# Converting weights to bf16 in HBM before they are streamed, and moving their loads from POOL to SP

## The chip, the cores and the metric

The kernel runs on the 8 cores of one Trainium2 chip, the same program on each. The metric is the device time in microseconds of the slowest core.

## What is computed

One transformer layer on x of shape (2, 4096, 4096) in float32: grouped-query attention with 32 query heads and 8 key/value heads of width 128, whose keys and values go through a narrow projection; then a feed-forward part with one dense 4096x4096 matrix and a top-2 mixture of 28 rank-8 adapters. Cut to what matters:

```python
def attn(u):
    q = heads(u @ Wq.T)                       # Wq 4096x4096
    kc, vc = u @ Wk_down.T, u @ Wv_down.T     # 4096 -> 256 each
    lat = interleave(kc, vc)                  # then k, v = up-projections
    k, v = lat[..., :256] @ Wk_up.T, lat[..., 256:] @ Wv_up.T
    p = softmax(causal(q @ k.T / sqrt(128)))
    return (p @ v) @ Wo.T                     # Wo 4096x4096
def ffn(u):
    logits = u @ gate_W.T                     # 28 experts, top 2
    h = (u @ lora_A.T) * gate(logits) * 2.0   # 28 x 8
    return u @ base_W.T + h @ lora_B.T        # base_W 4096x4096
x = x + layernorm(attn(layernorm(x)))
x = x + layernorm(ffn(layernorm(x)))
```

## The kernel before

Each core handles one of the two sequences together with three others, and owns 1024 of its 4096 rows as two halves of 512. It computes the compressed keys and values of all 4096 rows itself. All weights arrive as float32 in HBM, already laid out in blocks: WQ4 and WO4 as 32 blocks of [128, 4096], BWBM4 (base_W with lora_B appended) as 32 of [128, 4352], ATP (lora_A) as 32 of [128, 256], WKVD4 as 4 of [128, 4096]. Every such load is issued by POOL (`GPS`) and casts to bf16 on the way into SBUF. Waits are written out by hand on semaphores, and each engine runs its program in order.

The work has these stages:
- Keys and values, lines 247 to 283: eight blocks `ub` of 512 rows. For each: four tiles of X, layer norm on VectorE and ScalarE (`ln_stats_apply`, into the two-deep buffer UTM), four 1 MB transposes issued by SP (`tr_u`, L210) into UFMA or UFMA2; then `pa_loads(ub + 1)` queues the next X loads on POOL (L245); then four column groups `cg`, each a 1 MB WKVD4 load on POOL (L270) into WP[cg % 2] and 32 matmuls of 512 columns (L274), evacuated by VectorE.
- Then for each half `ci` of the own rows: layer norm and transposes of XOWN (L315, L323), Q projection over 32 groups `hdc` (load L330, matmuls L334), attention (L348 to L500), output projection over 32 groups `oc2` (load L540, matmuls L544) whose results SP transposes back (`tp_out2`, L534), two layer norms, gate, 32 small ATP loads with 4 matmuls each (L659, L665), and the FFN over 32 groups (load L709, 34 matmuls at L713 and L718, `tp_ffn` L703), with a last layer norm and the stores of OUT by SP (L754).

In all the weight loops the buffers WP[0] and WP[1] alternate: a load waits until the matmuls of the group two before it are done (`wp_free`), and the matmuls wait for the load. HSC is transposed by SP in four small transposes (L691) between the ATP loop and the FFN loop.

Of the kernel before, what the change touches and what calls it, by code (L numbers as in the profile page):

```python
# [7 lines left out]
BF16 = mybir.dt.bfloat16  # L8
# [51 lines left out]
def build(nc, do_b=True, do_c=True, dbg=False, dbg_stage=None):  # L60
# [4 lines left out]
    WQ4 = nc.dram_tensor("WQ4", [32, 128, 4096], F32, kind="ExternalInput").ap()  # L65
# [4 lines left out]
    WO4 = nc.dram_tensor("WO4", [32, 128, 4096], F32, kind="ExternalInput").ap()  # L70
    BWBM4 = nc.dram_tensor("BWBM4", [32, 128, 4352], F32, kind="ExternalInput").ap()
    GWT = nc.dram_tensor("GWT", [128, 896], F32, kind="ExternalInput").ap()
    ATP = nc.dram_tensor("ATP", [32, 128, 256], F32, kind="ExternalInput").ap()
    OUT = nc.dram_tensor("OUT", [1024, DM], F32, kind="ExternalOutput").ap()

    DBGT = None
    if dbg:
        DBGT = nc.dram_tensor("DBG", [512, DM], F32, kind="ExternalOutput").ap()
# [22 lines left out]
    WP = [A("WPa", [128, 34 * 128], BF16, O_WS), A("WPb", [128, 34 * 128], BF16, O_WP1)]  # L101
# [30 lines left out]
    TEN, VEC, SCA, GPS, SYN = nc.tensor, nc.vector, nc.scalar, nc.gpsimd, nc.sync  # L132

    tS = Sem(nc, "tS")
# [5 lines left out]
    sWPh = [Sem(nc, "sWPh0"), Sem(nc, "sWPh1")]  # L140
# [6 lines left out]
    sAP = [Sem(nc, "sAP0"), Sem(nc, "sAP1")]  # L147
    sST = Sem(nc, "sST")
    sSTp = [Sem(nc, "sSTa"), Sem(nc, "sSTb")]
    sRES = Sem(nc, "sRES")  # L150


    def W(eng, *sv):
        for s, v in sv:
            if v > 0:
                eng.wait_ge(s.h, v)
# [50 lines left out]
    def tr_u(dst, tspan, toff, utile, waits, pb):  # L207
# [4 lines left out]
    all_dma_sems = sXA + [sWPs[0], sWPs[1], sWPh[0], sWPh[1],  # L212
                    sTU[0], sTU[1], sTH[0], sTH[1],
                    sTP, sTHR, sWKV, sGW[0], sGW[1], sAP[0], sAP[1], sST, sRES,
                    sSTp[0], sSTp[1]]

    def final_waits():
        for s in all_dma_sems:
            if s.v > 0:
                SYN.wait_ge(s.h, s.v)  # L220


    Xr = X.rearrange("(q0 eight) d -> q0 eight d", eight=8)
    xu_extra = []
# [9 lines left out]
    wp_free = [0, 0]  # L234
# [13 lines left out]
    for ub in range(8):  # L248
        ubuf = UFMA if ub % 2 == 0 else UFMA2
        for t4 in range(4):  # L250
            pb = (ub * 4 + t4) % 6
            pl = (ub * 4 + t4) % 2
            xm = pend_xm[t4]
            xt = xa_tile(pb)
            ut = UTM[:, pl * 4096:(pl + 1) * 4096]
            ap_mark, red_mark = ln_stats_apply(
                xt, ut, pl,
                waits_v=[(sXA[pb], xm)],
                waits_s=[(sXA[pb], xm), (sTU[pl], utm_free[pl])])
            free_xa[pb] = (ap_mark, red_mark)  # L260
            tr_u(ubuf, 512, t4 * 128, ut,
                 [(sS, ap_mark), (tS, ufma_pa[ub % 2]), (vS, ufma_free_v)], pl)
            utm_free[pl] = sTU[pl].v
        if ub < 7:
            pa_loads(ub + 1)
        tp_all = [(sTU[0], sTU[0].v), (sTU[1], sTU[1].v)]
        for cg in range(4):
            wp = cg % 2
            W(GPS, (tS, wp_free[wp]))
            wm = sWPs[wp].inc(GPS.dma_start(out=WP[wp][:, 0:32 * 128], in_=WKVD4[cg]), 16)  # L270
            pp = cg % 2
            W(TEN, (sWPs[wp], wm), (vS, psab_free[pp]), *tp_all)
            for c in range(32):
                ins = TEN.matmul(PSab[pp][:], WP[wp][:, c * 128:(c + 1) * 128],  # L274
                                 ubuf[:, c * 512:(c + 1) * 512],
                                 start=(c == 0), stop=(c == 31))
            mm_mark = tS.inc(ins)
            wp_free[wp] = mm_mark
            if cg == 3:
                ufma_pa[ub % 2] = mm_mark  # L280
            W(VEC, (tS, mm_mark))
            psab_free[pp] = vS.inc(VEC.tensor_copy(  # L282
                KCVC[:, cg * 4096 + ub * 512:cg * 4096 + (ub + 1) * 512], PSab[pp][:]))
# [22 lines left out]
    for ci in range(2):  # L306
        nsl = 4 if ci == 0 else 8
        xbase = ci * 512
        for tt in range(4):
# [14 lines left out]
                 [(sS, ap_mark), (tS, ufma_free_t), (vS, ufma_free_v)], pl)  # L324
            utm_free[pl] = sTU[pl].v
        tp_all = [(sTU[0], sTU[0].v), (sTU[1], sTU[1].v)]
        for hdc in range(32):
            wp = hdc % 2
            W(GPS, (tS, wp_free[wp]))
            wm = sWPh[wp].inc(GPS.dma_start(out=WP[wp][:, 0:32 * 128], in_=WQ4[hdc]), 16)  # L330
            pp = hdc % 2
            W(TEN, (sWPh[wp], wm), (vS, psab_free[pp]), *tp_all)
            for c in range(32):
                ins = TEN.matmul(PSab[pp][:], WP[wp][:, c * 128:(c + 1) * 128],  # L334
                                 UFMA[:, c * 512:(c + 1) * 512],
                                 start=(c == 0), stop=(c == 31))
            mm_mark = tS.inc(ins)
            wp_free[wp] = mm_mark
            if hdc == 31:
                ufma_free_t = mm_mark  # L340
            W(VEC, (tS, mm_mark))
            if hdc == 0:
                W(VEC, *ostg_all)
            psab_free[pp] = vS.inc(VEC.tensor_copy(QFM[:, hdc * 512:(hdc + 1) * 512],
                                                   PSab[pp][:]))
# [190 lines left out]

        for oc2 in range(32):
            wp = oc2 % 2
            W(GPS, (tS, max(wp_free[wp], wo_base_free)))
            wm = sWPh[wp].inc(GPS.dma_start(out=WP[wp][:, 0:32 * 128], in_=WO4[oc2]), 16)  # L540
            pp = oc2 % 2
            W(TEN, (sWPh[wp], wm), (vS, max(psab_free[pp], attn_ready)))
            for hdc in range(32):
                ins = TEN.matmul(PSab[pp][:], WP[wp][:, hdc * 128:(hdc + 1) * 128],  # L544
                                 QFM[:, hdc * 512:(hdc + 1) * 512],
                                 start=(hdc == 0), stop=(hdc == 31))
            mm_mark = tS.inc(ins)
            wp_free[wp] = mm_mark
            if oc2 == 31:
                qfm_free_t = mm_mark  # L550
            W(VEC, (tS, mm_mark))
            em = vS.inc(VEC.tensor_copy(OUT2T[:, oc2 * 512:(oc2 + 1) * 512], PSab[pp][:]))
            psab_free[pp] = em
            evac_marks.append(em)
            if oc2 >= 2:
                tp_out2(oc2 - 2)
# [98 lines left out]
        ap_free = [wp_free[0], wp_free[0]]  # L655
        for c in range(32):
            ap2 = c % 2
            W(GPS, (tS, ap_free[ap2]))
            am = sAP[ap2].inc(GPS.dma_start(out=WP[0][:, ap2 * 256:(ap2 + 1) * 256],  # L659
                                            in_=ATP[c]), 16)  # L660
            W(TEN, (sAP[ap2], am))
            if c == 0:
                W(TEN, (sS, pss_free_s))
            for ts in range(4):
                ins = TEN.matmul(PSS[:, ts * 512: ts * 512 + 256],  # L665
                                 QFM[:, c * 512 + ts * 128: c * 512 + (ts + 1) * 128],
                                 WP[0][:, ap2 * 256:(ap2 + 1) * 256],
                                 start=(c == 0), stop=(c == 31))
            ap_free[ap2] = tS.inc(ins)
# [35 lines left out]

        for oc2 in range(32):
            wp = oc2 % 2
            W(GPS, (tS, max(wp_free[wp], bl_base_free)))
            wm = sWPh[wp].inc(GPS.dma_start(out=WP[wp][:], in_=BWBM4[oc2]), 16)  # L709
            pp = oc2 % 2  # L710
            W(TEN, (sWPh[wp], wm), (vS, psab_free[pp]))
            for c in range(32):
# [128 lines left out]
```

How the kernel before makes its waits and increments, by code:

```python
    def inc(self, ins, k=1):  # L54
        ins.then_inc(self.h, k)
        self.v += k
        return self.v
# [2 lines left out]
def build(nc, do_b=True, do_c=True, dbg=False, dbg_stage=None):  # L60
# [92 lines left out]
    def W(eng, *sv):  # L153
        for s, v in sv:
            if v > 0:
                eng.wait_ge(s.h, v)
# [60 lines left out]
    def final_waits():  # L217
        for s in all_dma_sems:
            if s.v > 0:
                SYN.wait_ge(s.h, s.v)
# [64 lines left out]
    x1_pa = [(tS, ufma_pa[1])]  # L285
    if not do_b:
        stm = 0
        for cc in range(4):
            W(VEC, (sST, stm))
            VEC.tensor_copy(OSTG[:], KCVC[:, cc * 4096:(cc + 1) * 4096])
            dm = vS.inc(VEC.drain())
            W(SYN, (vS, dm))
            stm = sST.inc(SYN.dma_start(out=DBGT[cc * 128:(cc + 1) * 128, :], in_=OSTG[:]), 16)
            SYN.wait_ge(sST.h, stm)
        final_waits()
        return
# [103 lines left out]
                if dbg_stage == "kv0" and ci == 0 and hg == 0 and sl == 0:  # L402
                    stm = 0
                    DSTG = ACC[:, 0:2048]
                    for (src_t, row) in ((KFM, 0), (VTM, 128)):
                        W(VEC, (sST, stm), (vS, upv_done))
                        VEC.tensor_copy(DSTG, src_t[:, 0:2048])
                        dm = vS.inc(VEC.drain())
                        W(SYN, (vS, dm))
                        stm = sST.inc(SYN.dma_start(
                            out=DBGT[row:row + 128, 0:2048], in_=DSTG), 16)
                        SYN.wait_ge(sST.h, stm)
                    final_waits()
                    return
```

## Time and profile before

| | |
|---|---|
| time before, median of 2 runs | 4825.37 us (4818.99 to 4831.74) |
| the profiled execution, own time | 4833.49 us |
| its span on the slowest core (7) | 4832.3 us |
| spans of all cores | 4696.0 to 4832.3 us |
| PE (matmul) busy | 3079.3 us, 64% |
| VectorE / ScalarE busy | 1527.2 us / 1029.5 us |
| POOL's DMA queue | 302.50 MB, 36.2% of 16 engines' span |
| SP's DMA queue | 84.50 MB, 14.9% |
| HBM read / written | 604.93 MB / 16.78 MB |

Bytes of a queue are counted as they are written: a cast load of 1 MB has read 2 MB. The busy shares are means over stages that have different limits, so the table alone says little. The share of the DMA engines is that of the time their packets took. In the views, "DMA X<-Y" as the cause of a wait means that the transfer into X had not landed.

### The profile page before, as it was taken

The page shows a single profiled execution, that of the slowest core. Times are in us where ns is not written, and L with a number is a line of the kernel's source. Part 1 is how long each engine was busy: PE and PEld are TensorE (multiplying, and loading weights), DVE is VectorE, ACT ScalarE, POOL GpSimd, SP SyncE. Part 2 cuts the span into 40 slices and gives each one's busy share as a digit, 9 for nine tenths or more (in the row PEclk, how much of TensorE's full clock was granted, in tenths as well). Part 3 has the DMA queues.
Part 4 walks back from the last instruction along what each step waited for, and adds up shares of the span by engine and source line. Part 5 has one row for each costly group of instructions (what it writes and reads, how often), then busy time and mean ns, then how long its engine had stood idle before and what let it go on. Part 6 is the DMA issues. An engine that isn't in the chain of part 4 may idle for free.

```text
span 4832.3 us, 36425 instructions; the slowest of 8 cores (4696.0 to 4832.3 us)
## 1 busy us (share of the span) xinstructions
PE 3079.3 (64%) x13056; PEld 1195.7 (25%) x13056; DVE 1527.2 (32%) x2250; ACT 1029.5 (21%) x977; POOL 193.3 (4%) x358
## 2 busy tenths in 40 slices
PE   2211222458698897843884387899889997843883
PEld 0100111123232232311331133233223332311331
DVE  2221222220065662032003200566666661032003
ACT  1111011210055450011001100455545550011001
POOL 0000000000000000001000000000000000001000
PEclk9655666679899998975997699999999998975997
DMA  8999999676710006833774766200000006733774
GB/s 145 109 85 90 85 103 101 110 146 124 132 23 1 1 1 108 144 65 59 130 143 106 145 117 116 58 1 1 1 1 1 1 1 116 138 62 64 130 140 121
DMA packets 322733, 389.32 MB, mean 81 GB/s; under 512 B 276208, under 2 KB 284656, under 8 KB 284672
## 3 DMA queue, kind: packets, MB, share of 16 engines
q0 software_dynamic: 49856, 302.50, 36.2%
q1 hardware_dynamic: 272704, 84.50, 14.9%
q8 instruction: 110, 1.80, 0.2%
q14 instruction: 63, 0.52, 0.0%
HBM read 604.93 MB, written 16.78 MB: 129 GB/s over the span
## 4 chain that ended last, share of the span: by engine, by line
PE 47%; DMA 25%; DVE 8%; another core or an unknown queue 6%; ACT 5%; issue 4%; SPq 3%; DVEq 1%; POOLq 1%; ACTq 0%; POOL 0%
PE psz L425 8%; PE pss L460 6%; PE psa L334 5%; DMA WPb<-BWBM 4%; DMA WPa<-WO 4%; DMA WPa<-WQ 4%; PE psb L713 4%; DVE BSTAT L186 4%; PE psb L432 4%; PE psa L432 4%; PE psa L544 4%; DMA UFMA<-UTM 3%; SPq L210 3%; PE psa L274 3%
## 5 line engine op out<-in xcount | busy, mean ns | idle before, releaser
L468 ACT ACTIVATE PTD<-pss 128x1024 bf16<-128x1024 f32 x768 | 740.8, 1021 | 667.6 <-PE pss L460 667.6
L474 DVE TENSOR_TENSOR PTD<-PTD,M 128x2048 bf16<-128x2048 bf16 x384 | 470.4, 1225 | 420.1 <-ACT PTD L468 420.1
L274 PE MATMUL psa<-UFMA,WPa 128*128 128x512 bf16 x512 | 134.1, 428 | 733.1 <-DMA UFMA<-UTM 709.5
L460 PE MATMUL pss<-QFM,KFM 128*128 128x512 bf16 x1536 | 403.5, 380 | 68.4 <-ACT PTD L468 45.7
L334 PE MATMUL psa<-UFMA,WPa 128*128 128x512 bf16 x1024 | 252.9, 410 | 239.9 <-DMA UFMA<-UTM 173.9
L425 PE MATMUL psz<-PTD,E 128*16 128x512 bf16 x1536 | 396.4, 381 | 0.2 <-DVE ACC L447 0.2
L198 ACT ACT_TABLE_LOAD x5 | 6.4, 1283 | 1382.5 <-DVEq L196 1382.5
L544 PE MATMUL psa<-QFM,WPa 128*128 128x512 bf16 x1024 | 232.8, 387 | 69.9 <-DMA WPa<-WO 68.1
L713 PE MATMUL psb<-QFM,WPb 128*128 128x512 bf16 x1024 | 239.6, 395 | 57.5 <-DMA WPb<-BWBM 55.5
L713 PE MATMUL psa<-QFM,WPa 128*128 128x512 bf16 x1024 | 234.9, 389 | 48.4 <-DMA WPa<-BWBM 46.4
L274 PEld LDWEIGHTS psa<-UFMA,WPa 128*128 128x128 bf16 x512 | 53.9, 107 | 812.8 <-issue 768.3
L544 PE MATMUL psb<-QFM,WPb 128*128 128x512 bf16 x1024 | 226.1, 379 | 26.7 <-DMA WPb<-WO 21.0
L334 PE MATMUL psb<-UFMA,WPb 128*128 128x512 bf16 x1024 | 227.9, 381 | 15.1 <-DMA WPb<-WQ 10.7
L198 ACT ACTIVATE STAT<-STAT 128x1 f32<-128x1 f32 x64 | 12.9, 202 | 1028.8 <-DVEq L196 569.1
L282 DVE CAST KCVC<-psa 128x512 bf16<-128x512 f32 x16 | 11.1, 692 | 642.7 <-PE psa L274 642.7
L460 PEld LDWEIGHTS pss<-QFM,KFM 128*128 128x128 bf16 x1536 | 142.2, 98 | 278.1 <-issue 125.2
L186 DVE BATCH_NORM_STATS2 BSTAT<-XA 128x6 f32<-128x512 bf16 x320 | 193.7, 678 | 33.0 <-DMA XA<-XOWN 14.6
L334 PEld LDWEIGHTS psa<-UFMA,WPa 128*128 128x128 bf16 x1024 | 104.4, 104 | 388.2 <-issue 290.2
L432 PE MATMUL psb<-PTD,VTM 128*128 128x512 bf16 x768 | 199.2, 382 | 0.0
L432 PE MATMUL psa<-PTD,VTM 128*128 128x512 bf16 x768 | 199.1, 382 | 0.0
L425 PEld LDWEIGHTS psz<-PTD,E 128*16 128x16 bf16 x1536 | 106.4, 88 | 261.1 <-issue 164.7
L202 ACT ACTIVATE UTM<-XA,STAT 128x4096 bf16<-128x4096 bf16 x40 | 152.0, 3800 | 2.8
(119 smaller groups left out, 2459.1 us busy)
## 6 DMA issues: line engine op xcount, KB each, us to landing
WPa<-BWBM POOLq DMA_DIRECT2D x32, 1088.0 KB, 9.0
WPb<-BWBM POOLq DMA_DIRECT2D x32, 1088.0 KB, 9.6
XA<-X POOLq DMA_DIRECT2D x32, 1024.0 KB, 20.9
WPa<-WQ POOLq DMA_DIRECT2D x32, 1024.0 KB, 8.5
WPb<-WQ POOLq DMA_DIRECT2D x32, 1024.0 KB, 8.4
WPa<-WO POOLq DMA_DIRECT2D x32, 1024.0 KB, 8.6
WPb<-WO POOLq DMA_DIRECT2D x32, 1024.0 KB, 8.8
WPa<-WKVD POOLq DMA_DIRECT2D x16, 1024.0 KB, 10.0
```

Of the source, the lines that this page charges most:

```text
L186: VEC.bn_stats(BS[:, i * 6:(i + 1) * 6], src_tile[:, i * 512:(i + 1) * 512])
L202: ins = SCA.activation(utile, src_tile, AF.Identity, bias=Snmr, scale=Sr)
L210: return sTU[pb].inc(SYN.dma_start(out=ap, in_=utile, transpose=True), 16)
L274: ins = TEN.matmul(PSab[pp][:], WP[wp][:, c * 128:(c + 1) * 128], ubuf[:, c * 512:(c + 1) * 512], start=(c == 0), stop=(c == 31))
L334: ins = TEN.matmul(PSab[pp][:], WP[wp][:, c * 128:(c + 1) * 128], UFMA[:, c * 512:(c + 1) * 512], start=(c == 0), stop=(c == 31))
L425: TEN.matmul(PSZ[0:16, :], E16[:, ph4 * 16:(ph4 + 1) * 16], PTD[:, pptp * 2048 + kt * 512: pptp * 2048 + (kt + 1) * 512], start=(sl == 0 a ...
L432: ins = TEN.matmul(PSab[avb][:], VTM[:, kt * 512 + pkv4 * 128: kt * 512 + (pkv4 + 1) * 128], PTD[:, pptp * 2048 + kt * 512: pptp * 2048 + ...
L460: ins = TEN.matmul(PSS[:, kt * 512:(kt + 1) * 512], KFM[:, kv4 * 512 + kt * 128: kv4 * 512 + (kt + 1) * 128], QFM[:, h * 512:(h + 1) * 512 ...
L468: ins = SCA.activation(PTD[:, ptp * 2048 + hf2 * 1024: ptp * 2048 + (hf2 + 1) * 1024], PSS[:, hf2 * 1024:(hf2 + 1) * 1024], AF.Exp, scale= ...
L474: pm = vS.inc(VEC.tensor_tensor(PTD[:, ptp * 2048:(ptp + 1) * 2048], PTD[:, ptp * 2048:(ptp + 1) * 2048], M01[:], AL.mult))
L544: ins = TEN.matmul(PSab[pp][:], WP[wp][:, hdc * 128:(hdc + 1) * 128], QFM[:, hdc * 512:(hdc + 1) * 512], start=(hdc == 0), stop=(hdc == 31))
L713: TEN.matmul(PSab[pp][:], WP[wp][:, c * 128:(c + 1) * 128], QFM[:, c * 512:(c + 1) * 512], start=(c == 0), stop=False)
```

## The change

Five tensors in HBM are added. POOL issues DMAs that read float32 blocks from HBM and write them to HBM as bf16: 12 in each of the eight blocks of the first stage, ahead of the third column group's load (POOL first waits for WP[0]'s last matmuls, those of the first group), in the order WQ, WO, BWBM; these are 96. The 32 of ATP follow in the first half, behind the four XOWN loads. The loads of WQ, WO, BWBM and ATP blocks into SBUF now read the bf16 tensors, and are issued by SP with a wait for all conversions of their kind. WKVDB and its semaphore are declared and not used. WKVD, the up-projections, X and XOWN are loaded as before.

```diff
+    WQB = nc.dram_tensor("WQB", [32, 128, 4096], BF16, kind="Internal").ap()
+    WOB = nc.dram_tensor("WOB", [32, 128, 4096], BF16, kind="Internal").ap()
+    BWBMB = nc.dram_tensor("BWBMB", [32, 128, 4352], BF16, kind="Internal").ap()
+    ATPB = nc.dram_tensor("ATPB", [32, 128, 256], BF16, kind="Internal").ap()
...
+    conv_jobs = []
+    for i in range(32):
+        conv_jobs.append((sCVQ, WQB[i], WQ4[i]))
+    for i in range(32):
+        conv_jobs.append((sCVO, WOB[i], WO4[i]))
+    for i in range(32):
+        conv_jobs.append((sCVB, BWBMB[i], BWBM4[i]))
+    for i in range(32):
+        conv_jobs.append((sCVA, ATPB[i], ATP[i]))
+    cv_i = [0]
+
+    def pump_conv(n):
+        for _ in range(n):
+            if cv_i[0] >= len(conv_jobs):
+                return
+            s, d, srcp = conv_jobs[cv_i[0]]
+            s.inc(GPS.dma_start(out=d, in_=srcp), 16)
+            cv_i[0] += 1
...
@@ in the loop over cg, after the matmuls
+            if cg == 1:
+                W(GPS, (tS, wp_free[0]))
+                pump_conv(12)
...
@@ in the loop over ci, after the transposes of XOWN
+        pump_conv(len(conv_jobs))
         for hdc in range(32):
             wp = hdc % 2
-            W(GPS, (tS, wp_free[wp]))
-            wm = sWPh[wp].inc(GPS.dma_start(out=WP[wp][:, 0:32 * 128], in_=WQ4[hdc]), 16)
+            W(SYN, (tS, wp_free[wp]), (sCVQ, sCVQ.v))
+            wm = sWPh[wp].inc(SYN.dma_start(out=WP[wp][:, 0:32 * 128], in_=WQB[hdc]), 16)
...
-            W(GPS, (tS, max(wp_free[wp], wo_base_free)))
-            wm = sWPh[wp].inc(GPS.dma_start(out=WP[wp][:, 0:32 * 128], in_=WO4[oc2]), 16)
+            W(SYN, (tS, max(wp_free[wp], wo_base_free)), (sCVO, sCVO.v))
+            wm = sWPh[wp].inc(SYN.dma_start(out=WP[wp][:, 0:32 * 128], in_=WOB[oc2]), 16)
...
-            W(GPS, (tS, ap_free[ap2]))
-            am = sAP[ap2].inc(GPS.dma_start(out=WP[0][:, ap2 * 256:(ap2 + 1) * 256],
-                                            in_=ATP[c]), 16)
+            W(SYN, (tS, ap_free[ap2]), (sCVA, sCVA.v))
+            am = sAP[ap2].inc(SYN.dma_start(out=WP[0][:, ap2 * 256:(ap2 + 1) * 256],
+                                            in_=ATPB[c]), 16)
...
-            W(GPS, (tS, max(wp_free[wp], bl_base_free)))
-            wm = sWPh[wp].inc(GPS.dma_start(out=WP[wp][:], in_=BWBM4[oc2]), 16)
+            W(SYN, (tS, max(wp_free[wp], bl_base_free)), (sCVB, sCVB.v))
+            wm = sWPh[wp].inc(SYN.dma_start(out=WP[wp][:], in_=BWBMB[oc2]), 16)
```

## Rows read from the trace of the kernel before

**Rows 1.** The page, the span in 40 slices of 121 us: busy tenths.

```profile
PE   2211222458698897843884387899889997843883
DMA  8999999676710006833774766200000006733774
```

**Rows 2.** Busy time by stretch of the span, the first stage; columns in the header.

```profile
core 7: us, PE busy (x) PEld busy (x) DVE busy (x) ACT busy (x) POOL busy (x), PEclk, DMA share, GB/s
0.00:980.00 980.00, 244.52 (x1022) 103.55 (x1023) 203.13 (x417) 138.57 (x97) 38.93 (x77) 0.68 0.94 105
```

**Rows 3.** Timeline, end of the first block: start, duration, instruction [idle before <- releaser].

```profile
99.42 0.53 POOL L270 DMA_DIRECT2D WPa<-WKVD  x1 [64.93 <-PE psa L274]
...
106.33 0.53 POOL L270 DMA_DIRECT2D WPb<-WKVD  x1 [6.37 <-PE psb L274]
106.85 1.06 POOL L245 DMA_DIRECT2D XA<-X  x2
110.09 8.75 PE L274 MATMUL psa<-UFMA,WPa 128*128 128x512 bf16 x32 [4.30 <-DMA WPa<-WKVD]
...
126.60 4.83 DVE L186 BATCH_NORM_STATS2 BSTAT<-XA 128x6 f32<-128x512 bf16 x8
```

**Rows 4.** The 1 MB transposes of L210: who waited for them, and time to landing.

```profile
  PE psa L274: 709.5, 8
...
DMA to landing us min/median/max: 5.6/5.7/78.5
```

**Rows 5.** The same line from 900 to 1030 us: who waited.

```profile
  PE psa L334: 46.2, 1
```

**Rows 6.** Chain that ended last, start of the first Q stage: start, duration, what.

```profile
1026.85 9.75 PE psa L334 x32
...
1037.13 7.75 DMA WPa<-WQ
...
1045.34 7.08 PE psa L334 x32
...
1095.45 8.94 DMA WPb<-WQ
```

**Rows 7.** By stretch, columns as in rows 2: Q, WO, FFN, Q, WO, FFN.

```profile
1026.80:1300.00 273.20, 235.21 (x1024) 100.71 (x1024) 21.51 (x32) 0.00 (x0) 15.83 (x30) 0.96 0.65 116
1848.20:2112.20 264.00, 227.54 (x1024) 98.39 (x1024) 21.95 (x32) 0.00 (x0) 16.90 (x32) 0.99 0.78 139
2298.00:2597.00 299.00, 252.42 (x1088) 107.86 (x1088) 22.59 (x35) 0.00 (x0) 15.81 (x30) 0.95 0.74 129
2724.60:3011.00 286.40, 242.97 (x1024) 103.03 (x1024) 21.44 (x31) 0.00 (x0) 15.84 (x30) 0.92 0.63 110
4015.30:4283.30 268.00, 230.49 (x1024) 99.25 (x1024) 21.48 (x32) 0.00 (x0) 16.89 (x32) 0.98 0.77 136
4469.00:4761.50 292.50, 247.45 (x1088) 106.71 (x1088) 22.60 (x36) 0.00 (x0) 15.84 (x30) 0.97 0.74 133
```

**Rows 8.** By stretch, columns as in rows 2: eight or more loads queued on POOL.

```profile
30.00:80.00 50.00, 0.00 (x0) 0.00 (x0) 9.32 (x21) 6.70 (x5) 1.58 (x3) 1.00 1.03 176
```

**Rows 9.** The stores of OUT, 1 MB each, issued by SP.

```profile
L754 SPq DMA_DIRECT2D OUT<-OSTG x16: 332/332/353, 2614.7 to 4827.8; - x16
...
DMA to landing us min/median/max: 3.8/4.0/4.6
```

**Rows 10.** The loads of ATP (L659): who waited for them.

```profile
  PE pss L665: 89.9, 40
```

**Rows 11.** The 128 KB transposes of L534: time to landing.

```profile
DMA to landing us min/median/max: 2.3/8.7/10.5
```

**Rows 12.** DMA issues: size of each and median us to landing.

```profile
WPa<-ATP POOLq DMA_DIRECT2D x64, 64.0 KB, 3.3
```

**Rows 13.** Chain that ended last, first loads of the two WO stages.

```profile
1838.02 10.02 DMA WPa<-WO
...
4006.34 8.75 DMA WPa<-WO
```

More of the change, by code:

```diff
@@ L74, in build @@
     OUT = nc.dram_tensor("OUT", [1024, DM], F32, kind="ExternalOutput").ap()
+    WQB = nc.dram_tensor("WQB", [32, 128, 4096], BF16, kind="Internal").ap()
+    WOB = nc.dram_tensor("WOB", [32, 128, 4096], BF16, kind="Internal").ap()
+    BWBMB = nc.dram_tensor("BWBMB", [32, 128, 4352], BF16, kind="Internal").ap()
+    ATPB = nc.dram_tensor("ATPB", [32, 128, 256], BF16, kind="Internal").ap()
+    WKVDB = nc.dram_tensor("WKVDB", [4, 32, 128, 128], BF16, kind="Internal").ap()
     DBGT = None
@@ L150, in build @@
     sRES = Sem(nc, "sRES")
+    sCVQ = Sem(nc, "sCVQ")
+    sCVO = Sem(nc, "sCVO")
+    sCVB = Sem(nc, "sCVB")
+    sCVA = Sem(nc, "sCVA")
+    sCVK = Sem(nc, "sCVK")
     def W(eng, *sv):
@@ L214, in build @@
                     sTP, sTHR, sWKV, sGW[0], sGW[1], sAP[0], sAP[1], sST, sRES,
-                    sSTp[0], sSTp[1]]
+                    sSTp[0], sSTp[1], sCVQ, sCVO, sCVB, sCVA, sCVK]
     def final_waits():
```

## The prediction

> **What bounds the kernel now.** I read the page's slices first, to see that the run is made of stages with different limits: TensorE (PE) at 2 to 4 tenths with the DMA engines at 8 or 9 for the first fifth of the span, then PE at 8 or 9 [rows 1]. The table by stretch says it in microseconds [rows 2]. The projection of keys and values (the loop `ub`, lines 248 to 283) takes the first 980 us, with the DMA share at 0.94 and PE busy for only 244.5 us. The attention stages have almost no DMA in the slices and are not touched by the change. What is left is the six weight-streaming stages, Q (L334), WO (L544) and FFN (L713), twice each.
>
> The timeline of the end of the first block [rows 3] shows the order in the `ub` loop, which matters most here. After the first column group POOL issues the load for the third (99.42), after the second the load for the fourth (106.33), and at once two X loads. VectorE starts the next block's statistics only after both groups are evacuated (126.60). The transposes of that next block come after that. So from 99.4 on, the chain is load, matmul, matmul, layer norm, transposes, and nothing of the next block runs ahead of it but X loads. PE's long waits are for transposes, 709.5 us in 8 pieces [rows 4].
>
> The six weight stages are two-deep rings: a load can start only when the buffer's matmuls are done, and must land while the other buffer is multiplied. A group of 32 matmuls takes 7.08 us once the clock is up, the load 7.8 to 8.9 us, so the chain alternates between the two [rows 6]. The stages' whole lengths stand in [rows 7].
>
> **The change, part by part.**
>
> *1. 96 conversions in the first stage.* Twelve DMAs per block go to POOL's queue right behind the first column group, each reading 2.10 MB of float32 from HBM and writing 1.05 MB of bf16 back. The 32 of BWBM are 1/16 larger, so the work is 98 units. The queue is served in order, as far as this trace shows, and the third group's load is issued behind the twelve. In [rows 3] everything after 99.42 hangs on that load. The conversions are therefore not hidden: no transpose is pending, PE has one group left (7 us), and layer norm waits behind the fourth group. No row shows a DMA from HBM to HBM, so I bound one from both sides. Below: loads queued back to back moved 176 GB/s of bf16 [rows 8], so 1.05/176 = 6.0 us for a unit, if the write rides for nothing beside the read. Above: a store of 1 MB to HBM lands in 4.0 us [rows 9]; fully in series that gives 10.0 us. Between them: if bytes at HBM are the limit, the same stream reads 2 x 176 = 352 GB/s, and a conversion moves 3.15 MB, so 3.15/352 = 8.9 us. I take 8.9, because read and write together in 6.0 us would need 3.15/6.0 = 525 GB/s per core, half more than any row shows. 98 x 8.9 = +872 us.
>
> The Trainium skill (HBM Reference, section Specifications (TRN2)) gives about 358 GB/s per core when both cores of a pair stream. The trace's 352 GB/s agrees; by the page's figure, an estimate, the conversion would be 3.15/358 = 8.8 us and the sum some 10 us less.
>
> *2. What the queue gives back there.* Before, from 99.4 to 125.9 the load and two groups took 26.5 us. Afterwards the third load streams behind the conversions (6.0 us, no start-up), and the fourth is queued behind it, so 6.0 + 7.1 + 7.1 = 20.2. That is 6 us less in each of 8 blocks: -48.
>
> *3. The 32 ATP conversions* go to POOL behind the four XOWN loads of the first half. POOL needs 32 x 0.53 = 17 us to issue them (its issues in [rows 3]), and each is 1/16 unit, 0.6 us by the price above. They run beside layer norm and four transposes, which they can delay, and take the place of two 1 MB loads. I take +10, ends 0 and 35 (17 + 18).
>
> *4. Q, WO and FFN loads in bf16 from SP.* Half the bytes, no cast. No row shows such a load. The nearest is the 1 MB store from SP, landing in 4.0 us [rows 9]; above stands the present load, 7.8 to 8.9 us [rows 6]. I take 4.0, nearest in bytes and queue. What matters is only that it is below 7.08 us: then each stage is PE-bound. Q or WO: first group 9.75 us (the clock starts low), then 31 x 7.1 = 220, together 230. FFN has 34 matmuls a group: 9.6 + 31 x 7.7 = 248. From [rows 7]: 273.2 + 264.0 + 286.4 + 268.0 - 4 x 230 = 172, and 299.0 + 292.5 - 2 x 248 = 95; together -267.
>
> The new waits stand in SP's program, so I looked at what queues behind them. A load for group n waits for group n-2; behind it stands the output transpose of group n-2, which waits for that group's evacuation anyway. The next load is due a whole group (7 us) later. Nothing is late. The waits on the conversion counters pass at once, since these finished stages before.
>
> *5. Starts of the stages.* WO's first load is now issued while attention runs, because SP isn't held by POOL's wait for the last multiply: -(10.0 + 8.75) = -19 [rows 13]. Q's first load is now queued behind SP's four transposes and FFN's behind the four small HSC transposes: up to one load (4.0 us) later each, but those transposes no longer share the engines with two 1 MB loads of POOL's. I set both at nothing, ends -20 and +20.
>
> *6. ATP from SP.* PE waits 89.9 us in all [rows 10] on 64 loads of 3.3 us [rows 12]. The smallest SP transfer of the trace, a 128 KB transpose, lands in 2.3 us at best [rows 11]; with that, each of 16 pairs in a stage is 1.0 us shorter. The first pair is no longer prefetched, because SP first has the transpose of the logits: 4 us lost. Twice (16 - 4): -24, ends 0 and -50.
>
> Sum: 872 - 48 + 10 - 267 - 19 - 24 = +524. The profiled execution took 4833.5 us (span 4832.3), 0.2% above the median of the runs. 4833.5 + 524 = **5357 us**, slower by 11%.
>
> **Rivals.**
>
> *The write is free (20%).* A conversion costs as much as a load, 6.0 us. For it: DMA engines that are the limit on their reading side would do this, and the stream's 176 GB/s may be that limit. Against it: 525 GB/s at HBM. 98 x 6.0 = 588; the sum is +240, 5073 us.
>
> *Conversions dearer, or weight loads not hidden (24%).* At 10.0 us per unit the sum is +632, 5465 us. If instead the bf16 loads took over 7.1 us (SP's transposes share their queue now), the 267 us would be gone: +791, 5624 us. The point is a landing of 7.1 us. Against the latter: the store's 4.0.
>
> *Faster: the slow transposes are cured (2%).* The eight PE waits in the first stage average 709.5/8 = 89 us [rows 4]; the same four transposes cost PE 46.2 us before the first Q stage [rows 5]. One landed 78.5 us after its issue, the median is 5.7 [rows 4]. If the new order kept them apart from POOL's loads, 8 x 43 = 340 us would come back. With the 6.0 us conversion: 240 - 340 = -100, 4733 us, 2.1% faster. It needs both, and a conversion of at most 6.0 us for more than 2%. Against it: the X loads and the first two weight loads of each block are released at the same points as before, so they meet the transposes as before. The Trainium skill (DMA: Bandwidth & Descriptors, section Queues, rings and completion order) says that an engine alternates between its queues packet by packet, which fits transposes that crawl beside large-packet loads. By that rule a backlog of conversions would make them crawl too, but by the program they never meet in the first stage.
>
> *The change does not act as written* (conversions spread out over the idle attention stages, so that they are hidden): they are all issued and drained before the first Q stage by POOL's order, so under 2%.
>
> **How the numbers follow.** Likeliest: 5357 us, 52%, own range 5290 to 5430 (a unit at 8.3 to 9.6 us). Write free: 5073, 20%. Dearer or loads not hidden: 5465 and above, 24%. Transposes cured, or conversions hidden: 4%, of which half ends inside 2%. The range from 5045 to 5500 takes in the free write and the serial bound of 10.0, and leaves out a tenth above and a few hundredths below. About 2% is what a measurement of this kernel can tell from no change: faster 1%, within 2% 3%, slower 96%.
>
> **What would show it.** Right: the first stage grows from 980 to about 1800 us, with twelve DMAs ahead of each third group's load, some 107 us per block; DMA share near 1 there with PE idle; the third group waiting on WKVD and not on transposes; Q and WO stages of about 230 us and FFN of 248, with no PE wait on WQ, WO or BWBM and landings of 4 to 5 us. Wrong: a block growing by only 72 us (a free write) or by 120 and more; PE still waiting on weights in the six stages; or the transposes' 709.5 us changed by more than 100.

## The result, and the profile after

The changed kernel takes 5258.8 us (median of 11 runs, 5227.9 to 5384.5) against 4835.7 us for the kernel before on the same chips (median of 10). The ratio is 1.087, 95% interval 1.081 to 1.092: slower by 8.7%. Forecast were 5357 us.

In some executions of every kernel here one die of the chip has a lower granted clock and is some per cent longer; ratios leave such executions out, and the others are called undisturbed below.

The tables compare core 7 with core 7 of before (the core of [rows 2, 7]); its span is 5160.5 us against 4832.3, +328. It is not the slowest core of the profiled execution: that is core 3 with 5329.6 us, +497 over the slowest of before. The difference lies in the first stage, which ends at 1669.7 us on core 7 and at 1841.4 on core 3; from the first Q matmul on, all eight cores need 3427 to 3452 us.

The stretches of after, columns as in [rows 2]: first stage, then Q, WO, FFN, Q, WO, FFN.

```profile
core 7: us, PE busy (x) PEld busy (x) DVE busy (x) ACT busy (x) POOL busy (x), PEclk, DMA share, GB/s
0.00:1670.00 1670.00, 256.76 (x1024) 106.87 (x1024) 203.37 (x418) 138.47 (x97) 101.06 (x204) 0.60 0.95 124
1714.80:1939.30 224.50, 223.44 (x1024) 100.42 (x1024) 21.43 (x31) 0.00 (x0) 0.00 (x0) 0.99 0.42 142
2474.90:2700.40 225.50, 224.01 (x1024) 100.60 (x1024) 21.43 (x31) 0.00 (x0) 0.55 (x1) 0.99 0.55 159
2878.90:3115.50 236.60, 236.57 (x1087) 106.80 (x1088) 21.43 (x31) 0.00 (x0) 0.00 (x0) 0.99 0.55 162
3237.20:3461.40 224.20, 223.59 (x1024) 100.30 (x1024) 21.43 (x31) 0.00 (x0) 0.00 (x0) 0.99 0.40 142
4453.10:4676.00 222.90, 222.76 (x1024) 100.43 (x1024) 21.45 (x32) 0.00 (x0) 0.55 (x1) 0.99 0.54 161
4852.60:5088.90 236.30, 236.28 (x1088) 106.65 (x1088) 21.43 (x31) 0.00 (x0) 0.00 (x0) 0.99 0.55 162
```

The first stage has grown by 70% with the same 1024 matmuls in it, and its DMA share stays at 0.95. The six weight stages are now matmul and nothing else: PE busy equals the length of the stretch to 1.5 us or less, at a granted clock of 0.99, where [rows 7] had 36 to 47 us of idle PE in each. What each part came to, core 7, from the first and last matmul of each stage:

| part | forecast | measured |
|---|---|---|
| first stage ends | +824 (872 - 48) | 980.7 to 1669.7: +689 |
| from there to the first Q matmul | +10 | 46.2 to 45.2: -1 |
| Q and WO stages, four | -172 | 273.0+263.3+286.3+267.8 to 224.4+225.5+224.2+222.8: -193 |
| FFN stages, two | -95 | 298.5+291.8 to 236.5+236.2: -118 |
| WO starts (idle before the first matmul) | -19 | 12.6+10.9 to 1.3+0.9: -21 |
| ATP loops, with the gap before them | -24 | 148.6 to 113.9, gaps +12: -23 |
| second Q start, FFN starts | 0 | 128.1 to 121.7; 9.1+9.7 to 13.1+12.1: 0 |
| attention, two | 0 | 512.4+969.9 to 510.7+967.3: -4 |
| sum | +524 | +328 |

The timeline of the first block of after, PE and POOL, beside which stands [rows 3] of before:

```profile
99.46 5.84 POOL L246 DMA_DIRECT2D WQB<-WQ  x12 [65.02 <-PE psa L300]
105.27 0.59 POOL L296 DMA_DIRECT2D WPa<-WKVD  x1
106.39 0.54 POOL L296 DMA_DIRECT2D WPb<-WKVD  x1 [0.53 <-PE psb L300]
106.92 1.07 POOL L271 DMA_DIRECT2D XA<-X  x2
224.38 8.47 PE L300 MATMUL psa<-UFMA,WPa 128*128 128x512 bf16 x32 [118.55 <-DMA WPa<-WKVD]
```

POOL issues twelve conversions and the third group's load within 7 us, and the third group starts 118.6 us later: the load waits behind all twelve. Over the stage, what ended PE's waits at the first-stage matmuls (us, times) is this:

```profile
  DMA WPa<-WKVD: 726.9, 8
  DMA UFMA<-UTM: 686.0, 8
```

The first line was this in the kernel before:

```profile
  DMA WPa<-WKVD: 23.6, 8
```

The second answers [rows 4] and is nearly as it was (709.5): the change added its 689 us as a new wait and took only 24 from the old one. The weight loads (issues: size, median us from issue to landing) land in 4.8 to 5.7 us and are not waited for inside a stage. Only the first load of each Q and FFN stage ends a wait (166.5 us in two pieces, 25.2 in two); the waits before Q, 173.9 us, were ended by the transposes before.

```profile
WPa<-WQB SPq DMA_DIRECT2D x32, 1024.0 KB, 4.9
WPa<-WOB SPq DMA_DIRECT2D x32, 1024.0 KB, 5.2
WPa<-BWBMB SPq DMA_DIRECT2D x32, 1088.0 KB, 5.5
```

### The profile page after: what moved, and what is told of

It is laid out like the page before. It is cut to its first block, busy times and chain, and to the rows that moved or that the text cites. A ratio compares the mean times of both kernels' runs of the same rounds, so it can differ in the third digit from the quotient of the medians.

```text
span 5329.6 us, 36821 instructions; the slowest of 8 cores (5060.7 to 5329.6 us)
## 1 busy us (share of the span) xinstructions
PE 3028.8 (57%) x13056; PEld 1199.9 (23%) x13056; DVE 1527.7 (29%) x2250; ACT 1029.6 (19%) x977; POOL 121.1 (2%) x230
## 4 chain that ended last, share of the span: by engine, by line
PE 54%; another core or an unknown queue 19%; DMA 9%; DVE 6%; ACT 5%; SPq 3%; issue 2%; DVEq 1%; POOLq 0%; ACTq 0%; POOL 0%
PE psz L455 7%; PE pss L490 6%; DMA UFMA<-UTM 5%; PE psa L364 4%; PE psb L743 4%; PE psb L574 4%; PE psa L574 4%; PE psb L364 4%; PE psa L743 4%; PE psa L462 3%; PE psb L462 3%; SPq L218 3%; DVE BSTAT L194 3%; PE psa L300 3%
## 5 line engine op out<-in xcount | busy, mean ns | idle before, releaser
L300 PE MATMUL psa<-UFMA,WPa 128*128 128x512 bf16 x512 | 146.4, 457 | 1584.1 <-DMA WPa<-WKVD 927.8
L490 PE MATMUL pss<-QFM,KFM 128*128 128x512 bf16 x1536 | 403.6, 380 | 68.5 <-ACT PTD L498 45.8
L743 PE MATMUL psb<-QFM,WPb 128*128 128x512 bf16 x1024 | 226.2, 379 | 0.7 <-DMA WPb<-BWBMB 0.7
L574 PE MATMUL psb<-QFM,WPb 128*128 128x512 bf16 x1024 | 226.2, 379 | 0.5 <-DMA WPb<-WOB 0.5
L210 ACT ACTIVATE UTM<-XA,STAT 128x4096 bf16<-128x4096 bf16 x40 | 152.0, 3800 | 2.8
```

The lines of the kernel that those rows point to most:

```text
L210: ins = SCA.activation(utile, src_tile, AF.Identity, bias=Snmr, scale=Sr)
L490: ins = TEN.matmul(PSS[:, kt * 512:(kt + 1) * 512], KFM[:, kv4 * 512 + kt * 128: kv4 * 512 + (kt + 1) * 128], QFM[:, h * 512:(h + 1) * 512 ...
L743: TEN.matmul(PSab[pp][:], WP[wp][:, c * 128:(c + 1) * 128], QFM[:, c * 512:(c + 1) * 512], start=(c == 0), stop=False)
```

## Experiments

**The price of a conversion by itself (e1 and e2).** A program of its own, with six phases of twelve transfers of 1 MB written, each phase drained before the next; once on all 8 cores, once on a single one.

```python
for i in range(12): G.dma_start(out=CONVA[i], in_=SRC[i])        # f32 HBM -> bf16 HBM
for i in range(12): G.dma_start(out=CAST[...], in_=SRC[i])       # f32 HBM -> bf16 SBUF
for i in range(12): G.dma_start(out=CONVP[i][:, 0:4096], in_=SRC[i])  # padded rows
for i in range(12): S.dma_start(out=COPY[i], in_=CONVA[i])       # bf16 HBM -> HBM
for i in range(12): S.dma_start(out=CAST[...], in_=CONVA[i])     # bf16 HBM -> SBUF
for i in range(12): S.dma_start(out=STORE[i], in_=CAST[...])     # bf16 SBUF -> HBM
```

> A program that computes nothing of the layer: on all 8 cores, six phases of twelve DMAs queued back to back, one after the other: (1) float32 in HBM to bf16 in HBM, contiguous blocks as in the changed kernel; (2) float32 in HBM to bf16 in SBUF; (3) as 1, with the bf16 rows in padded rows of 4352, so that no packet spans two rows; (4) bf16 HBM to HBM from SP; (5) bf16 HBM to SBUF from SP; (6) bf16 SBUF to HBM from SP. Then the output is filled. Theory (HBM bytes shared with other cores set the cost of a conversion): phase 1 takes about 12 x 9.7 = 116 us here, phase 3 the same, phase 2 about 12 x 6.0 = 72 us; the same program on one core alone takes about 12 x 6 for phases 1 and 3. Rival (a DMA from HBM to HBM costs the engines 9.7 us per MB whoever else runs, or the 32 KB packets do): phase 1 takes 116 us on one core too; if it is the packet size, phase 3 is shorter than phase 1 on both.

> The same six phases on one core, the other seven idle. Theory (shared HBM): phases 1 and 3 take about 72 us (6.0 us per block), phase 2 60 to 72 us. Rival (cost of the DMA engines or of the packets): phase 1 takes 116 us as with eight cores.

The timeline of the eight-core program, core 6; a phase lasts from its own first line's start to the next one's:

```profile
1.53 5.96 POOL L26 DMA_DIRECT2D CONVA<-SRC  x12 [0.83 <-POOLq L60]
118.17 6.37 POOL L30 DMA_DIRECT2D CAST<-SRC  x12 [110.68 <-DMA CONVA<-SRC]
196.98 6.12 POOL L34 DMA_DIRECT2D CONVP<-SRC  x12 [72.44 <-DMA CAST<-SRC]
312.15 12.22 SPq L38 DMA_DIRECT2D COPY<-CONVA  x12
387.68 10.91 SPq L42 DMA_DIRECT2D CAST<-CONVA  x12
427.53 13.24 SPq L46 DMA_DIRECT2D STORE<-CAST  x12
463.65 8.31 SPq L53 DMA_DIRECT2D OUT<-FIN  x8
```

The same of the single core:

```profile
1.48 5.95 POOL L26 DMA_DIRECT2D CONVA<-SRC  x12 [0.78 <-POOLq L60]
62.95 6.37 POOL L30 DMA_DIRECT2D CAST<-SRC  x12 [55.53 <-DMA CONVA<-SRC]
124.87 6.16 POOL L34 DMA_DIRECT2D CONVP<-SRC  x12 [55.54 <-DMA CAST<-SRC]
186.07 7.52 SPq L38 DMA_DIRECT2D COPY<-CONVA  x12
226.33 8.03 SPq L42 DMA_DIRECT2D CAST<-CONVA  x12
```

With eight cores a conversion costs (118.17 - 1.53)/12 = 9.7 us and a cast load 78.8/12 = 6.6; their bytes at HBM are 3.15 and 2.10 MB, so both run at 318 to 325 GB/s per core. The bf16 copy, 2.10 MB, takes 6.3 us (333 GB/s). So the price goes by bytes at HBM, as the prediction's step had it, at a rate 8% below its 352. With one core the conversion takes 5.1 us, the cast load 5.2: the write does ride for nothing, at 614 GB/s. Padded rows cost the same on both (9.6 and 5.1 us), so it is not the packets either. Both mechanisms of the prediction exist, then, and which one holds depends on who else is at the memory. The bf16 load takes 3.3 us with eight cores and 2.7 with one. The Trainium skill (HBM Reference, section Specifications (TRN2)) gives about 358 GB/s per core when both cores of a pair stream, and this case's eight-core phases stay under it, at 318 to 333 where data is read.

**Why 7.5 us and not 9.7 in the kernel.** The table takes the time from the issue of a block's first conversion to the third group's start, in the trace of after. By the two programs it should be 116.6 + 6.6 = 123 us if both cores of a pair convert at once and 61.5 + 5.2 = 67 if the core is alone.

| core | block 1 | 2 | 3 | 4 | 5 | 6 | 7 | 8 |
|---|---|---|---|---|---|---|---|---|
| 6 | 122.7 | 110.0 | 71.2 | 72.1 | 78.4 | 83.8 | 79.1 | 95.3 |
| 7 | 124.9 | 120.4 | 90.3 | 85.3 | 78.5 | 89.2 | 91.5 | 97.8 |
| 2 | 125.3 | 122.7 | 120.5 | 121.2 | 108.9 | 118.6 | 116.1 | 112.0 |
| 3 | 123.0 | 125.0 | 113.4 | 125.1 | 118.6 | 125.5 | 123.0 | 125.2 |

The timeline lines behind three of these figures, POOL's issues and PE's third group, of core 6, then of 7, then of 3:

```profile
core 6 of [0, 1, 2, 3, 4, 5, 6, 7], span 5060.7 us
...
541.13 3.89 POOL L246 DMA_DIRECT2D WQB<-WQ  x8 [72.58 <-PE psa L300]
...
612.36 9.93 PE L300 MATMUL psa<-UFMA,WPa 128*128 128x512 bf16 x32 [64.85 <-DMA WPa<-WKVD]
...
core 7 of [0, 1, 2, 3, 4, 5, 6, 7], span 5160.5 us
...
601.06 3.89 POOL L246 DMA_DIRECT2D WQB<-WQ  x8 [106.80 <-PE psa L300]
...
691.38 8.78 PE L300 MATMUL psa<-UFMA,WPa 128*128 128x512 bf16 x32 [83.94 <-DMA WPa<-WKVD]
...
core 3 of [0, 1, 2, 3, 4, 5, 6, 7], span 5329.6 us
...
1514.63 5.89 POOL L246 DMA_DIRECT2D BWBMB<-BWBM  x12 [82.08 <-PE psa L300]
...
1637.66 9.44 PE L300 MATMUL psa<-UFMA,WPa 128*128 128x512 bf16 x32 [116.65 <-DMA WPa<-WKVD]
```

Cores 6 and 7 start together (98.2 and 99.5), and in the first two blocks pay the price of two. By the third block core 6 is through (541 to 612) when core 7 begins (601 to 691), and each pays 71 to 98 us from then on. Cores 2 and 3 stay in step through all eight blocks (their seventh batches start at 1497 and 1515) and pay 109 to 126 every time. Over the 64 blocks of the 8 cores, with 0-1, 2-3, 4-5, 6-7 as pairs, and a batch counted up to 5 us before the third group's start, the 20 blocks whose batch overlaps the partner's by under a tenth average 83.8 us, the 23 that overlap by over eight tenths 121; the correlation of time and overlap is 0.93, and the overlap with the six other cores adds nothing to it in a fit of both. On cores 4 to 7 alone it is 0.91, and over the 64 blocks of e3 below, another execution with the same conversions, 0.91 too (22 blocks average 81.9 us, 19 average 119.9). A pair shares what limits the conversions, and whether the two fall out of step decides up to 40 us per block. The price of a pair in step also shows in the spans of another execution of after, of 5344.4 us: cores 0 and 1 have 5309 and 5343, no other core over 5216. No run forced a pair out of step, so this rests on the traces and on the two ends.

**Only the conversions, the loads as before (e3).** Against after:

```diff
-            W(SYN, (tS, wp_free[wp]), (sCVQ, sCVQ.v))
-            wm = sWPh[wp].inc(SYN.dma_start(out=WP[wp][:, 0:32 * 128], in_=WQB[hdc]), 16)
+            W(GPS, (tS, wp_free[wp]))
+            wm = sWPh[wp].inc(GPS.dma_start(out=WP[wp][:, 0:32 * 128], in_=WQ4[hdc]), 16)
```

and likewise for WO, BWBM and ATP.

> The changed kernel with its 128 conversions as they are, but all weight loads as before (float32, issued by POOL): the conversions' result is not used. Theory: the first stage grows by about 690 us as in the changed kernel and nothing is given back: 4836 + 700 = about 5535 us, ratio 1.145. Rival (the first stage grew for another reason, such as SP's loads or their waits, and the conversions hide partly): well below, 5250 or less.

Measured: 5617.6 us, ratio 1.164 (1.148 to 1.180), more than the 1.145 expected. Core 7's first stage, columns as in [rows 2]:

```profile
0.00:1740.00 1740.00, 257.09 (x1024) 106.97 (x1024) 203.21 (x417) 138.67 (x97) 101.58 (x205) 0.60 0.95 118
```

The first Q stage is again 279.0 us long and the later ones are as before. The whole loss is the first stage's, and somewhat larger than in after; its waits on WKVD are 826.2 us on core 7, between those of cores 4 to 7 of after (661.5 to 783.2) and those of its cores 2 and 3, which stayed in step (894.4 and 927.8). Core 7 and its partner fell out of step later here: its eight batches sum to 877 us, against 778 in after.

**Only the cheap loads (e4, e5).** One block each of WQ, WO and BWBM is converted, and every group loads block 0, by SP as in the change (e4) or by POOL (e5); ATP is converted whole. All the other blocks of the three weights are left out of the computation.

```diff
-    for i in range(32):
+    for i in range(1):
         conv_jobs.append((sCVQ, WQB[i], WQ4[i]))
...
-            wm = sWPh[wp].inc(SYN.dma_start(out=WP[wp][:, 0:32 * 128], in_=WQB[hdc]), 16)
+            wm = sWPh[wp].inc(SYN.dma_start(out=WP[wp][:, 0:32 * 128], in_=WQB[0]), 16)
```

> The changed kernel's loads of WQ, WO, BWBM and ATP in bf16 from SP, with one block each of WQ, WO and BWBM converted instead of 32, and every group loading that block (so all groups use block 0's weights); ATP is converted whole. Theory: gives back what the changed kernel's later stages gave, 361 us on core 7, less some 30 for 3 blocks and ATP in the first stages: 4836 - 330 = about 4505 us, ratio 0.932. Rival (the later stages gained from something that the conversions bring): a gain well under 250 us.

> As the run that loads only block 0 of each converted tensor, but with those bf16 loads issued by POOL and not by SP. It tells the two halves of the edit apart: fewer bytes, or another queue. Theory (bytes): a bf16 load from POOL lands in 5 to 6 us, still below a group's 7.1 us, so the stages stay PE-bound; lost against SP's loads are only WO's early first load (2 x 10 us) and the quicker ATP loads (2 x 12): about 4560 us against 4516. Rival (it was the queue: POOL's descriptors or casts cost): landings near 8 us and about 4780 us.

Undisturbed executions took 4514.2 and 4518.9 us with SP's loads and 4509.7 and 4523.7 with POOL's (medians of all four: 4685.8 and 4551.3); POOL's ratio is 0.935 (0.928 to 0.941). Landings are 4.9, 5.3 and 5.4 us from SP against 5.1, 5.5 and 5.9 from POOL; the Q, WO and FFN stages take 223.5, 224.1 and 237.9 us against 225.8, 227.1 and 240.4. Almost all of the gain behind the first stage is in the halved bytes. The change of queue is worth 2 to 3 us a stage, and 24 us on core 7 from the first Q matmul on (3472.2 to 3448.2); the times don't show it. Both runs still pay for three conversions: core 7's first stage ends at 1028.7 us in e4 and not at 980.7. Had the bf16 weights come for nothing, the kernel would be some 7.5% faster, by the 360 us that core 7 gives back behind the first Q matmul in after (3805.4 to 3445.6).

**The conversions a little later (e11).** In the change the twelve are issued behind the fourth group's load instead of ahead of the third's.

```diff
-            if cg == 1:
-                W(GPS, (tS, wp_free[0]))
+            if cg == 3:
                 pump_conv(12)
```

> The changed kernel with its twelve conversions per block issued after the fourth column group's load and not after the second's matmuls, so that they run beside the next block's layer norm and transposes instead of ahead of the third group's load. Theory (the first stage is bound by DMA and HBM in either place, and transposes crawl behind POOL's large packets): the wait moves from the third group's load to the transposes, and the run takes 5220 to 5330 us as the changed kernel does. Rival (the place in the queue was the mistake, and the conversions hide behind layer norm and the matmuls): 5000 us or less. A third outcome, transposes that crawl beyond the conversions' own time: 5400 us or more.

One execution of four was undisturbed, the profiled one, and took 5129.5 us (median of all four 5334.0). Its waits at the first-stage matmuls, core 7:

```profile
  DMA UFMA<-UTM: 1205.3, 8
  DMA WPa<-WKVD: 19.5, 8
```

The wait has moved to the transposes, which now land up to 143 us after their issue; on core 7 the two lines sum to 1224.8 us against 1412.9 in after. How much comes back depends on the core. Here all eight stay in step (their first batches start between 106 and 108 us, the seventh between 1294 and 1303) and reach the first Q matmul between 1671 and 1678 us. In after they reach it between 1634 (core 6) and 1889 (core 3): core 7 gains 37 us and the slowest core 211. The time says so too, as far as one undisturbed execution can: 5129.5 us is below all thirteen executions of after on record, the least of which took 5204.2, and is 1.05 to 1.07 of the kernel before on the same chip (4815.7 to 4878.1), where after stands at 1.087. In all four executions of e11 cores 4 to 7, an undisturbed die, took at most 5126 to 5132 us; in after the slowest of them took 5186 or more. So the theory of "5220 to 5330 us" missed, and so did the rival of 5000: the place in the queue is worth some 75 to 140 us of the 423, and most of the price stays. Within the first stage there is no place that is free; its DMA share is 0.93 here, 0.94 in before and 0.95 in after.

**The order of POOL in the first stage (e7), to test the rival of the slow transposes.** The kernel before, without any conversion; the X loads wait until the transposes have landed, and the next block's first two WKVD loads are issued early.

```diff
-        if ub < 7:
-            pa_loads(ub + 1)
         tp_all = [(sTU[0], sTU[0].v), (sTU[1], sTU[1].v)]
+        if ub < 7:
+            W(GPS, *tp_all)
+            pa_loads(ub + 1, (0, 1, 2, 3) if ub == 0 else (2, 3))
...
+            if cg < 2:
+                w_load(cg + 2)
+            elif ub < 7:
+                w_load(cg - 2)
+            if cg == 1 and ub < 6:
+                pa_loads(ub + 2, (0, 1))
```

> The kernel before, no conversions, with only POOL's order in the first stage changed: while a block's transposes run, POOL issues nothing; the X loads wait for the transposes' landing, and the first two WKVD loads of the next block are issued as soon as their buffers are free. It tests the rival that slow transposes hold the first stage. If POOL's loads are what slows them, four transposes and their layer norm take 36 us as before the last block, and the block is then bound by 48 us of loads or by PE: 122 us fall to 75 to 85, so 980 us fall to about 680 to 720 and the run to about 4560, ratio 0.94. If they are slow for another reason, PE's waits for transposes stay at 90 us a block and the ratio is 0.98 to 1.02.

Core 7's first stage, then what PE waited for in it, then the landings of all transposes into UFMA:

```profile
0.00:643.00 643.00, 256.21 (x1024) 106.74 (x1024) 203.18 (x417) 138.92 (x97) 38.90 (x77) 0.75 0.88 160
```

```profile
  DMA UFMA<-UTM: 318.3, 8
```

```profile
DMA to landing us min/median/max: 5.6/5.7/23.7
```

The stage falls from 980 to 643 us on core 7: 337 come back, where the rival had put 340 (over the eight cores it ended at 881 to 981 us and now ends at 614 to 648). The transposes' waits go from 709.5 to 318.3 us and the slowest landing from 78.5 to 23.7. Two undisturbed executions took 4478.1 and 4482.8 us, those of before 4802 to 4852: 7% less. The run changes two things at once, the later X loads and the earlier WKVD loads; but PE's waits on WKVD into WP[0] grew, from 23.6 to 68.5 us, so the gain is the transposes'. The mechanism of that rival was real, and the change did not touch it.

**The conversions under attention (e6, e9).** From before: the conversions of WO and WQ are issued eight at a time among the slices of the first attention, those of BWBM and ATP in the second attention. Both WO stages load bf16, and so do Q, ATP and FFN in the second half; in the first half these three run from float32 as they did.

```diff
+                W(GPS, (vS, mask_mark))
+                if ci == 0:
+                    pump_conv(conv_jobs, 8)
+                else:
+                    pump_conv(late_jobs, 4 if len(late_jobs) > 32 else 8)
```

> The kernel before, with the conversions put where DMA is idle: WO and WQ in the eight slices of the first half's attention, 8 blocks at the start of each, BWBM and ATP in the second half's. So both WO stages, and the second half's Q, ATP and FFN stages load bf16 from SP; the first half's Q, ATP and FFN stay as before, and nothing is converted in the first stage. Theory (a conversion costs only where DMA is the limit): attention keeps its 512 and 970 us, and the stages give back what they gave in the changed kernel: 49 + 68 + 55 + 53 + 12 = 237 us, so about 4600 us, ratio 0.951. Rival (POOL's work or HBM traffic slows attention, or conversions spill into the WO stage): attention over 530 us in the first half, ratio above 0.97.

4728.4 us, ratio 0.975 (0.969 to 0.981), half of what was hoped; whether it is 2% stays open by that interval. The first attention, and the longest link of the chain in it:

```profile
1270.50:1902.00 631.50, 448.24 (x1824) 148.42 (x1824) 317.94 (x385) 248.21 (x257) 31.12 (x58) 0.86 0.93 116
```

```profile
1504.58 78.33 POOLq L509
```

Attention takes 631.5 us instead of 512. Line 509 is POOL's drain behind an iota, on which the end of a group of heads waits; it stood 78.3 us, and 53.8 at its second place, while POOL's conversions were in flight, and ended 3.8 and 1.7 us after their last packet had moved (at 1579.1 and 1883.7 us). In the kernel before, without conversions, VectorE waited 2.3 us for the same iota and drain. In e9 the iota raises the semaphore itself:

```diff
-            GPS.iota(IND16[:].rearrange("p (h m) -> p h m", h=16, m=128),
-                     pattern=[[1, 16], [0, 128]], base=0, channel_multiplier=-1,
-                     allow_small_or_imprecise_dtypes=True)
-            ind_g = gS.inc(GPS.drain())
+            ind_g = gS.inc(GPS.iota(IND16[:].rearrange("p (h m) -> p h m", h=16, m=128),
+                                    pattern=[[1, 16], [0, 128]], base=0, channel_multiplier=-1,
+                                    allow_small_or_imprecise_dtypes=True))
```

> The kernel with the conversions hidden in attention lost 100 to 120 us in the first half's attention; its profile shows POOL's drain behind the iota at the end of each head group waiting 78 and 54 us while conversions are in flight. Here the iota itself raises the semaphore and the drain is gone; nothing else differs. Theory (POOL's drain waits for the DMAs that POOL has issued, and everything else of attention is untouched): the first half's attention falls from 632 (core 7) to about 515 to 525 us, and the run to about 4610 us, ratio 0.951. Rival (the conversions slow attention through HBM, SBUF or POOL's issue): attention stays at 600 us or more, and the ratio at 0.975.

4716.8 us, ratio 0.971 (0.966 to 0.977). The drain was the cause: attention is back at 502 us, and on all eight cores the time from the end of Q to WO, 643 to 686 us in e6, is 530 to 542. But the gain moved on. Attention and the first WO stage, then who waited for what at WO's matmuls:

```profile
1298.40:1800.40 502.00, 447.01 (x1824) 148.02 (x1824) 317.92 (x385) 248.40 (x257) 31.11 (x58) 0.96 1.00 114
1801.70:2142.20 340.50, 228.28 (x1024) 101.56 (x1024) 21.44 (x31) 0.00 (x0) 1.61 (x3) 0.82 0.73 153
```

```profile
  DMA WPb<-WOB: 78.8, 2
  DMA WPa<-WOB: 33.9, 1
```

The attention has a DMA share of 1.00 now: 64 conversions at 9.7 us are 621 us, and it offers 502. On core 7 their packets move from 1326.8 to 1935.4 us, 9.5 us for each, and so 135 us past the end of attention. The rest of them runs beside WO, whose first loads then land late; the stage takes 340.5 us instead of 225.

**Both together (e8, e10), and what fits (e12).** e8 is e6 with the order of e7, e10 is e9 with it. e12 is e10 with 48 conversions instead of 64 in the first attention, six a slice; the last 16 groups of the second Q stage are loaded in float32 by POOL.

```diff
-    conv_jobs += [(sCVQ, WQB[i], WQ4[i]) for i in range(32)]
+    conv_jobs += [(sCVQ, WQB[i], WQ4[i]) for i in range(16)]
...
-            if ci == 0:
+            if ci == 0 or hdc >= 16:
...
-                    pump_conv(conv_jobs, 8)
+                    pump_conv(conv_jobs, 6)
```

> Both together: conversions in attention and the order of the first stage. The two touch different stages, so the theory has them add up: 4840 - 237 - 280 = about 4320 us, ratio 0.893. If either gain hangs on the other, it is less by that much.

> Conversions in attention without the drain, and POOL's new order in the first stage. From 0.911 with the drain, minus 115 us of 4845: ratio 0.887, about 4300 us. If the drain is not the cause, 0.91.

> As the run with hidden conversions, new order and no drain, with 48 conversions in the first half's attention and not 64 (six per slice: WO's 32 and 16 of WQ; the second half's Q loads its other 16 groups as float32 from POOL). Theory (with 64 blocks at 9.7 us, 621 us, the conversions outlast the 503 us of attention, and the loads of the first WO stage crawl beside the rest): 48 x 9.7 = 466 us fit, the first WO stage falls from 352 to about 225 us, the second Q stage rises from 223 to about 248 us: about 100 us less, 4404 - 100 = about 4300 us, ratio 0.885. Rival (WO's first loads are late for another reason, such as SP's waits): the WO stage stays near 340 us, ratio 0.905 to 0.91.

Measured: e8 4455.4 us, ratio 0.911 (0.906 to 0.916), short of the 0.893 by about what attention has grown with the drain still in it (670 to 694 us from Q to WO, 547 to 552 before); e10 4403.7 us, 0.905 (0.900 to 0.910), short of the 0.887, with attention at 503.3 and the first WO stage at 351.8; e12 4289.5 us, **0.891 (0.887 to 0.896)**, the fastest of all. Its first stage, attention, WO, and second Q stage:

```profile
0.00:624.00 624.00, 250.50 (x1024) 105.38 (x1024) 203.53 (x418) 138.57 (x97) 38.89 (x77) 0.76 0.91 165
966.00:1469.50 503.50, 448.24 (x1824) 148.57 (x1824) 317.82 (x385) 248.38 (x257) 24.29 (x44) 0.95 0.83 113
1470.90:1695.50 224.60, 224.11 (x1024) 100.54 (x1024) 21.44 (x31) 0.00 (x0) 1.61 (x3) 0.99 0.54 160
2281.30:2538.00 256.70, 230.74 (x1024) 101.43 (x1024) 21.44 (x31) 0.00 (x0) 8.44 (x16) 0.97 0.54 124
```

48 conversions at 9.7 us are 466 us, below the 503, and on core 7 the last packet moves at 1443.1 us, before attention ends; WO is bound by its matmuls again. The half-float32 Q stage gives back 32 us, which is the price of leaving 16 blocks out.

## Why the prediction was right, and by how much it was off

- **Direction and mechanism: right.** The third load waits behind twelve conversions, the third group's wait is on WKVD, and the transposes' 709.5 us moved by 24 only. e3 has the loss alone, e4 the gain alone.
- **Item 1, the unit at 8.9 us, is the mis-sized term.** In the table of blocks, the eight figures of core 7 sum to 778 us; less 8 x 6.0 for the third loads (as item 2 counts them) that is 730 for 98 units, 7.5 us each against 8.9, or -142 of 872. Those of core 3, the slowest, sum to 979 us: 931 for the 98 units, 9.5 us each, +59. The step that failed is not the choice between write free and write paid but that the bound was taken as one number for all blocks. It is 9.7 us where both cores of a pair convert (e1: even above the 8.9) and 5.1 where one does (e2), and in this execution three of the four pairs fall out of step after two to four blocks. The metric is the slowest core, so it sees the worst pair: core 3 waited 927.8 us for WKVD where core 6 waited 661.5. That is why the time grew by 423 us, and by 497 in the profiled execution, though core 7 shows 328.
- **Item 2, -48:** 689 - 730 = -41 measured, of which 24 is the transposes. Close, partly for another reason.
- **Item 3, +10: -1** on core 7, just below its ends of 0 and 35; the 32 small conversions hide behind the transposes. On the even cores, which are ahead of their partners, the step to the first Q matmul grew by 15 to 23 us, but none of them is the slowest.
- **Item 4, -267, was -311.** Landings of 4.8 to 5.7 us instead of 4.0 changed nothing, as said, since they lie under a group's time. The 44 us more come from the group: the forecast took 7.1 us for each from durations of 7.08 [rows 6], but in a stage without waits groups start 6.9 us apart, while each is still shown with 7.07: the end of one lies under the start of the next. FFN's groups are (236.5 - 9.4)/31 = 7.3 us apart where 7.7 was taken.
- **Items 5 and 6: -19 against -21, -24 against -23,** and the two starts set at nothing came to nothing in sum (second Q -6, FFN +4 and +2).
- **Rivals.** "The write is free" is true of one core alone (5.1 us against 5.2 for a cast load) and not of a pair at work, and 6.0 us a unit was passed below in the kernel where a core had its pair's memory for itself (71 us for twelve and a load). "Dearer" holds for the pair in step: 9.7, and 9.5 on core 3. "Loads not hidden" never came near its turning point: 5.7 against 7.1. "Slow transposes cured" was priced rightly, 337 measured on core 7 against 340, and does need a new order of POOL's queue, which the change doesn't bring.
- **The range** held, 5259 in 5045 to 5500; the likeliest case's own range, 5290 to 5430, did not. That the forecast came within 98 us is in part luck: it knew one price for a conversion, and which mixture of 5.1 and 9.7 the slowest core pays changes from one execution to the next (5330.8 and 5344.4 us with a pair in step, 5227.9 at the least).

What stays open: what pulls a pair out of step, and why two cores of one execution and all cores of e11 stayed in it; and the size of e11's gain, which rests on one undisturbed execution.

## What to carry to other kernels

A tensor that is read twice moves more bytes with a conversion in HBM than without (read 2, write 1, then twice 1: five parts, against twice 2), so it pays only where the memory is idle; put it under a stage with a low DMA share, and count how many units that stage holds at the price of the full chip. Price a transfer by its bytes at HBM with all cores moving data, and take the price of a lone core as the other end. Where large DMAs are queued, look at what engines wait for behind them on the same queue, and whether transposes run beside them.

## What the runs showed of the hardware

- A cast from HBM to HBM is issued like a load and costs 5.1 us per 1 MB written on one core, 9.7 on eight at once; padded rows cost the same (9.6 and 5.1).
- A drain on POOL stood 78.3 us while POOL's own DMAs were in flight, until 3.8 us after their last packet, and the wait was gone when the iota raised the semaphore itself.
- The 1 MB transposes, 5.7 us in the median, landed up to 78.5 us after issue beside POOL's X and WKVD loads, up to 143 beside conversions (e11), and up to 23.7 once the X loads were kept apart.
- The two cores of a pair, with the same program, can fall out of step by up to 60 us within three blocks (three pairs of after did, one did not, and none in e11); each then finds more of the memory free. On core 7 the conversions cost 730 us so, where 98 at the 9.7 us of a pair in step would be 951.
